# Two blocks' shared down projection as seven-product pairs, and first-block weight mixes moved to a later place

## What is computed

```python
xn = _layernorm(x)
# part 1: of each token's 2752 gate values the half that is smallest in size is set to zero
s = silu(einsum('bsh,ih->bsi', xn, w_gate))           # I = 2752
_, idx = top_k(-abs(s), int(0.5 * I))
s = s with those positions set to 0, times einsum('bsh,ih->bsi', xn, w_up)
part1 = einsum('bsi,hi->bsh', s, w_down)              # 1024 wide
# part 2
h = relu(einsum('bsh,hi->bsi', xn, up_w)) ** 2        # hidden, 2048 wide
shared_out = einsum('bsi,ih->bsh', h, down_w)         # the shared down projection
latent = einsum('bsh,hl->bsl', xn, fc1_w)             # 512 wide
routed_out = einsum('bsl,lh->bsh', einsum('bsl,lm->bsm', latent, expert_w) * sum_of_top2, fc2_w)
part2 = layernorm(shared_out + routed_out) * gamma + beta
return x + part1 + part2
```

## Time and profile before

| | us |
|---|---|
| median of 3 runs (lowest, highest) | 2308.17 (2308.01, 2308.75) |
| the profiled execution | 2309.1 |
| its span in the profile | 2307.3 |

### The profile page before, as it was taken

One profiled execution on the slowest core, in us unless ns is written; L12 is line 12 of the kernel. 1 busy time (PEld: TensorE's weight loads), 2 busy tenths in 40 slices (PEclk: granted clock), 3 DMA queues, 4 the chain that ended last, 5 costly groups with the idle time before them and its releaser, 6 DMA issues.

```text
span 2307.3 us, 27055 instructions
## 1 busy us (share of the span) xinstructions
PE 2286.7 (99%) x10360; PEld 1902.2 (82%) x10360; DVE 1155.0 (50%) x1496; ACT 698.2 (30%) x1093; POOL 890.7 (39%) x662
## 2 busy tenths in 40 slices
PE   8989999999999999999999999999999999999999
PEld 6878888888888888888888888888888888888887
DVE  4432667757334457607434544932823544690560
ACT  3233554223333326201114323510212432531110
POOL 5445656677445533133015452223203445204300
PEclk9999999999999999999999999999999999999999
DMA  7999999868888876557668887557667888755755
GB/s 267 338 396 395 347 364 334 301 212 298 295 288 282 272 282 234 194 192 273 213 232 295 270 291 278 195 195 259 223 222 252 270 281 292 246 193 195 272 191 179
DMA packets 213411, 611.88 MB, mean 265 GB/s; under 512 B 22304, under 2 KB 31520, under 8 KB 210208
## 3 DMA queue, kind: packets, MB, share of 16 engines
q1 hardware_dynamic: 213280, 610.13, 76.1%
HBM read 466.32 MB, written 143.72 MB: 264 GB/s over the span
## 4 chain that ended last, share of the span: by engine, by line
PE 93%; DMA 3%; DVE 2%; SPq 1%; ACT 1%; issue 0%; POOL 0%; DVEq 0%; ACTq 0%
PE bank L1107 30%; PE bank L1109 30%; PE bank L1108 30%; PE bank L1127 2%; DMA mixed_w<-mixes 2%; DMA raw<-w_gate_dram 1%; PE bank L1118 1%; DMA w<-mixed_w 0%; DMA split_w<-w 0%; SPq L667 0%; DVE positive L1368 0%; SPq L663 0%; PE bank L1201 0%; PE bank L1200 0%; DVE mixes L1317 0%
## 5 line engine op out<-in xcount | busy, mean ns | idle before, releaser
L886 POOL TENSOR_TENSOR w<-raw,w 128x512 fp32r<-128x512 f32 (+1 forms) x196 | 281.8, 1446 | 203.6 <-ACT w L930 203.2
L1107 PE MATMUL bank<-w,prod_t 128*128 128x512 f32 x672 | 269.4, 401 | 0.0
L1109 PE MATMUL bank<-w,prod_t 128*128 128x512 f32 x672 | 262.9, 391 | 0.0
L1108 PE MATMUL bank<-w,prod_t 128*128 128x512 f32 x672 | 262.0, 390 | 0.0
L1107 PE MATMUL bank<-w,tok 128*128 128x512 f32 (+1 forms) x664 | 254.1, 383 | 6.9 <-POOL w L886 6.0
L1109 PE MATMUL bank<-w,tok 128*128 128x512 f32 (+1 forms) x664 | 253.2, 381 | 0.0
L1108 PE MATMUL bank<-w,tok 128*128 128x512 f32 (+1 forms) x664 | 253.2, 381 | 0.0
L1108 PE MATMUL bank<-tok,w 128*128 128x512 f32 x640 | 249.0, 389 | 0.0
L1109 PE MATMUL bank<-tok,w 128*128 128x512 f32 x640 | 249.0, 389 | 0.0
L1107 PE MATMUL bank<-tok,w 128*128 128x512 f32 x640 | 249.0, 389 | 0.0
L891 POOL TENSOR_TENSOR w<-w 128x512 fp32r<-128x512 f32 x114 | 167.5, 1492 | 183.0 <-ACT w L1069 182.8
(11 more groups left out here) (175 smaller groups left out, 4334.0 us busy)
## 6 DMA issues: line engine op xcount, KB each, us to landing
w<-split_w SPq DMA_DIRECT2D x480, 512.0 KB, 4.2
split_w<-w SPq DMA_DIRECT2D x184, 512.0 KB, 5.9
w<-mixed_w SPq DMA_DIRECT2D x144, 256.0 KB, 3.3
w_more<-split_w SPq DMA_DIRECT2D x72, 512.0 KB, 5.1
w_more<-mixed_w SPq DMA_DIRECT2D x96, 256.0 KB, 3.7
rows<-x_dram SPq DMA_DIRECT2D x32, 512.0 KB, 5.2
mixed_w<-own SPq DMA_DIRECT2D x12, 1024.0 KB, 6.5
spilled_u<-prod SPq DMA_DIRECT2D x12, 1024.0 KB, 8.0
```

Source lines behind the costliest of these rows:

```text
L886: pool.tensor_tensor(lo, words, hi, ALU.subtract).then_inc(lo_ready, 1)
L1107: pe.matmul(out, left[0], right[0], start=first, stop=False)
L1108: pe.matmul(out, left[0], right[1], start=False, stop=False)
L1109: return pe.matmul(out, left[1], right[0], start=False, stop=last)
```

## The change

1. In blocks 2 and 3 (`WIDE`) the shared down projection becomes two pairs, 5 and 6, by seven products in an order of their own (`SHARED_PRODUCTS`). Latent and routed come before them. The granules of such a block after the fifth pair: latent 148, hidden 0 at 156, routed 164 and 168, hidden 1 at 172, pair 5 at 180 to 207, hidden 2 and 3 at 208 and 216, pair 6 at 224 to 251, out 252 to 295. A pair's left operands are the hidden values of two groups: the even one gives A11 (and, with its other half, S1), the odd one A12 and A22. ACT cuts them out of PSUM (`cut_units`), DVE multiplies by the relu (`make_units`) and forms S1 to S4, ACT makes high halves (`upper_units`, `upper_early_sum`, `upper_late_sums`), POOL the low halves (`lower_units`), and DVE adds the seven products into `acc` (`read_shared`, 28 adds of 512 columns a pair). T4's low half is made on DVE. A product with 48 fewer matmuls a block results: 336 instead of 384. The search steps, the pick, the masks, the gated products, the turns of the last chunks, and the loads of spilled up values are placed anew.
2. Eight new mixed sets for these pairs are made in block 1, at granules 158 + 7 i: loads, `mix_shared` on DVE at + 5, store at + 6.
3. In block 0 the twelve own sets move from granules 4 + 11 i to 44 + 9 i; mix at + 5 and store at + 6 instead of + 6 and + 7. gamma and beta are loaded at granule 158 instead of 142.

The core of the diff:

```diff
 PAIRS = [(("gate", 0), ("gate", 1)), (("gate", 2), ("gate", 3)), (("gate", GC - 2), ("up", GC - 2)),
-         (("up", 0), ("up", 1)), (("up", 2), ("up", 3))]
+         (("up", 0), ("up", 1)), (("up", 2), ("up", 3)),
+         (("shared", 0), ("shared", 1)), (("shared", 2), ("shared", 3))]
 
 FAST = [0, 5, 5, 5]
+WIDE = [False, False, True, True]
+SHARED_PAIRS = [5, 6]
 FIRST_PAIRS = 2
 UP_PAIR, SPILLED = 2, (3, 4)
 PRODUCTS = ["A11 B11", "S2 T2", "A12 B21", "S1 T1", "S4 B22", "S3 T3", "A22 T4"]
+SHARED_PRODUCTS = ["A11 B11", "S3 T3", "A12 B21", "A22 T4", "S1 T1", "S2 T2", "S4 B22"]
+SHARED_TARGETS = {"A11 B11": (11, 12, 21, 22), "S3 T3": (21, 22), "A12 B21": (11,), "A22 T4": (21,),
+                  "S1 T1": (12, 22), "S2 T2": (12, 21, 22), "S4 B22": (12,)}
...
+_WIDE_STEPS = [*_middle[:2], *_middle[3:5], _middle[2], SHARED_PAIRS[0], *_middle[7:9], SHARED_PAIRS[1], *_last[-2:]]
...
+                for n, p in enumerate(SHARED_PAIRS):
+                    even, odd = (end[("hidden", 2 * n + i)] for i in range(2))
+                    begun = self.start[("hidden", 2 * n + 1)]
+                    self.units_cut_at.update({even + 2: (n, 0), odd + 8: (n, 1)})
+                    self.units_at.update({even + 2: (n, 0), odd + 1: (n, 1)})
+                    self.early_sum_at[begun + 2] = n
+                    self.units_hi_at.update({begun + 3: (n, 0), odd + 8: (n, 1)})
+                    self.early_hi_at[begun + 4] = n
+                    self.late_hi_at[odd + 9] = n
+                    self.units_lo_at.update({begun + 5: (n, "early"), odd + 8: (n, "A12"), odd + 10: (n, "A22"),
+                                             odd + 12: (n, "S1"), odd + 15: (n, "S2"), odd + 19: (n, "S4")})
...
-        self.search_end = steps_at[COUNTS + 1] + 3 * TILES + 1
-        self.pick_at = {steps_at[COUNTS + 1] + 3 * t: t for t in range(TILES)}
-        self.pick_from = steps_at[COUNTS + 1]
+        self.pick_from = self.start[("hidden", 2)] + 1 if wide else steps_at[COUNTS + 1]
+        self.search_end = self.pick_from + (2 if wide else 3) * TILES + 1
+        self.pick_at = {self.pick_from + (2 if wide else 3) * t: t for t in range(TILES)}
...
-OWN_FROM = {n: 4 + 11 * i for i, n in enumerate(OWN_SETS)}
+OWN_FROM = {n: 44 + 9 * i for i, n in enumerate(OWN_SETS)}
 OWN_LOADS = {at + i: (n, i) for n, at in OWN_FROM.items() for i in range(4)}
-OWN_AT = {at + 6: n for n, at in OWN_FROM.items()}
-OWN_STORES = {at + 7: n for n, at in OWN_FROM.items()}
-FIRST_NORM_LOAD = 142
+OWN_AT = {at + 5: n for n, at in OWN_FROM.items()}
+OWN_STORES = {at + 6: n for n, at in OWN_FROM.items()}
+FIRST_NORM_LOAD = 158
...
+SHARED_FROM = {n: 158 + 7 * i for i, n in enumerate(SHARED_SETS)}
+SHARED_LOADS = {at + i: (n, i) for n, at in SHARED_FROM.items() for i in range(4)}
+SHARED_AT = {at + 5: n for n, at in SHARED_FROM.items()}
+SHARED_STORES = {at + 6: n for n, at in SHARED_FROM.items()}
...
 def vector_makes(granule):
 
-    return PRODUCTS[granule.key[2]] == VECTOR_LO and granule.key[1] < SPILLED[0]
+    _, p, q = granule.key
+    return products(p)[q] == VECTOR_LO and (p < SPILLED[0] or p in SHARED_PAIRS)
...
+            def load_shared_mix(n, i):
+
+                p, k = n // HALF, n % HALF
+                if n > SHARED_SETS[0]:
+                    sp.wait_ge(shared_stored, 16 * (n - SHARED_SETS[0]))
+                else:
+                    sp.wait_ge(bank_filled, filled(1, ("fast", FAST[1] - 1, len(PRODUCTS) - 1, 1)))
+                src, width = words_of((PAIRS[p][i // 2], k + i % 2 * HALF))
+                sp.dma_start(shared_own[:, i, :], src).then_inc(shared_loaded, 16)
+
+            def store_shared_mix(n):
+                sp.wait_ge(shared_mixes, 4 * (n - SHARED_SETS[0]) + 4)
+                sp.dma_start(mixed_w[n].rearrange("i p n -> p i n"), shared_own[:, :, :]).then_inc(shared_stored, 16)
...
+                    elif n in SHARED_SETS:
+                        sp.wait_ge(shared_stored, 16 * (n - SHARED_SETS[0] + 1))
...
+            def lower_units(b, n, what):
+
+                at = shared_round(b, n)
+                if what == "early":
+                    hi, lo = UNIT_SLOT["A11"]
+                    pool.wait_ge(unit_summed, at * UNIT_SUMS + 1)
+                    pool.wait_ge(operand_hi, highs(b, "hidden", (2 * n + 1) * TILES))
+                    pool.tensor_tensor(unit_r[:, lo, :, :], unit_raw[:, lo, :, :], unit_r[:, hi, :, :],
+                                       ALU.subtract).then_inc(units_lo, 1)
+                    hi, lo = SUM_SLOT["S3"]
+                    pool.wait_ge(unit_sum_hi, at * UNIT_HIS + 1)
+                    pool.tensor_tensor(unit_sums_r[:, lo, :, :], unit_sums[:, EARLY_RAW, :, :], unit_sums_r[:, hi, :, :],
+                                       ALU.subtract).then_inc(units_lo, 1)
+                elif what == "A12":
+                    hi, lo = UNIT_SLOT[what]
+                    for k in range(HALF):
+                        pool.wait_ge(unit_summed, at * UNIT_SUMS + 1 + 2 * k + 2)
+                        pool.wait_ge(operand_hi, highs(b, "hidden", (2 * n + 1) * TILES + k + 1))
+                        pool.tensor_tensor(unit_r[:, lo, k, :], unit_raw[:, lo, k, :], unit_r[:, hi, k, :],
+                                           ALU.subtract).then_inc(units_lo, 1)
...
+            def cut_units(b, n, odd):
+
+                if n == 0 and not odd:
+                    for c in range(4):
+                        act.wait_ge(spilled[c], 16 * b)
+                for k in range(HALF):
+                    words = banks[bank_of(b, ("hidden", 2 * n + odd, k))][:, :].rearrange("p (h n) -> p h n", h=2)
+                    act.wait_ge(bank_filled, filled(b, ("hidden", 2 * n + odd, k)))
+                    act.activation(unit_raw[:, 3:6:2, k, :] if odd else unit_raw[:, 1:8:6, k, :], words,
+                                   ACT.Relu).then_inc(units_cut, 1)
+
+            def upper_units(b, n, odd):
+
+                for k in range(HALF):
+                    act.wait_ge(units_made, shared_round(b, n) * 2 * HALF + odd * HALF + k + 1)
+                    hi, words = ((unit_r[:, 2:5:2, k, :], unit_raw[:, 3:6:2, k, :]) if odd else
+                                 (unit_r[:, 0, k, :], unit_raw[:, 1, k, :]))
+                    act.activation(hi, words, ACT.Copy).then_inc(operand_hi, 1)
...
+                if p in SHARED_PAIRS:
+                    n = SHARED_PAIRS.index(p)
+                    if granule.opens or left == "A12":
+                        pe.wait_ge(units_lo, unit_lo(b, n, (left, k) if left == "A12" else left))
...
+            def make_units(b, n, odd):
+
+                at = shared_round(b, n)
+                for k in range(HALF):
+                    bank = bank_of(b, ("hidden", 2 * n + odd, k))
+                    words = banks[bank][:, :].rearrange("p (h n) -> p h n", h=2)
+                    out = unit_raw[:, 3:6:2, k, :] if odd else unit_raw[:, 1:8:6, k, :]
+                    dve.wait_ge(units_cut, at * 2 * HALF + odd * HALF + k + 1)
+                    dve.scalar_tensor_tensor(out=out, in0=words, scalar=0.0, in1=out, op0=ALU.max,
+                                             op1=ALU.mult).then_inc(bank_emptied[bank], 1)
+                    value = emptied(b, ("hidden", 2 * n + odd, k))[1]
+                    dve.wait_ge(bank_emptied[bank], value)
+                    dve.sem_inc(units_made, 1)
+                if not odd:
+                    return
+                a12, a22, s3 = unit_raw[:, 3, :, :], unit_raw[:, 5, :, :], unit_sums[:, EARLY_RAW, :, :]
+                s4 = unit_sums[:, SUM_SLOT["S4"][1], :, :]
+                dve.wait_ge(units_lo, unit_lo(b, n, "S3"))
+                for k in range(HALF):
+                    dve.tensor_tensor(s3[:, k, :], a22[:, k, :], s3[:, k, :], ALU.subtract).then_inc(unit_summed, 1)
+                    dve.wait_ge(unit_summed, at * UNIT_SUMS + 1 + 2 * k + 1)
+                    dve.tensor_tensor(s4[:, k, :], a12[:, k, :], s3[:, k, :], ALU.subtract).then_inc(unit_summed, 1)
+                dve.tensor_tensor(unit_raw[:, 7, :, :], unit_raw[:, 7, :, :], a22, ALU.add).then_inc(unit_summed, 1)
...
+            def read_shared(b, p, q):
+
+                for j in range(2):
+                    bank, value = emptied(b, ("fast", p, q, j))
+                    dve.wait_ge(bank_filled, filled(b, ("fast", p, q, j)))
+                    if q or p > SHARED_PAIRS[0]:
+                        added = ("fast", p, q - 1, j) if q else ("fast", p - 1, 6, j)
+                        added_bank, added_value = emptied(b, added)
+                        dve.wait_ge(bank_emptied[added_bank], added_value)
+                    targets = SHARED_TARGETS[SHARED_PRODUCTS[q]]
+                    for target in targets:
+                        t, i = j + 2 * (target // 20), target % 10 - 1
+                        if p == SHARED_PAIRS[0] and q == 0:
+                            other, other_value = emptied(b, ("routed", i, t))
```

(4 more changed lines are left out.)

203 lines of the change are left out of this document (174 added, 29 removed).

## The result

The changed kernel takes 2346.10 us (median of 4 runs, 2344.37 to 2348.38) against 2308.09 of the kernel before (4 runs): a ratio of 1.0164, 95% interval 1.0151 to 1.0177. The forecast was 2308.9, with 2291 to 2325 as its range.

What follows compares the result with a forecast made beforehand. PE, busy 99%, was taken to bound the kernel: 2309.1 - 21.8 (matmuls) + 28 (four pairs) - 6.5 (block 0) + 1 (block 1) = 2309.8, less 0.9 to the median, 2308.9 us; range 2291 to 2325.

Steps and rivals of the forecast that it cites:

- Matmuls, -21.8: Shared down projection of the two wide blocks: 96 fewer matmuls at 0.2267 us each, -21.8 us, all on PE's path.
- T4's wait, 5.1 at first: Near granule 12 of each pair: PE waits for T4's low half, 3.7 to 6.5 us, taken as 5.1.
- E+22.8: Latest T4 time in a pair, counted from PE ending hidden 1 or 3; a wait of 6.5 us.
- My step that ACT's queue sets T4's time: Pair start: ACT's odd cut stands behind four mixed splits, free at about E+6.2, starting the chain to T4 at E+20.0.
- The second gap, 1.9: Between the second and third T4 low half DVE reads four banks: 1.1 to 2 us more, 1.9 taken per pair.
- the two don't add: In a pair, the second gap and half clock overlap, because a slow PE also needs T4's third low half later.
- 1.3 inside the same wait: Pair 6: six gated products on POOL, about 8.3 us, delay A12's low halves some 1.3 us, inside T4's wait.
- The out stage at nothing: Rest of the wide block, outside the pairs, costed at nothing; no term for the out stage.
- Block 0, -6.5: Moved own sets: -8.7 us of early waits and half clock, +1.2 near granule 154, +1 for stores; range -10.5 to 0.
- Block 1, +1: Eight shared sets through DVE and SP at granules 158 to 213 cost +1 us, range 0 to 5.
- B: Slower rival: POOL and DVE collide at every pair, half clock after each wait; 9.5 a pair, 38; 2318.9 us; chance 0.24.
- E's block 0: Slower rival through SP: stores hold SP, block 0 gives back nothing, block 1 loses 5; 2319.4 us; chance 0.05.

Runs made afterwards that it cites:

- no_gated: Changed kernel, with the six gated products on POOL ahead of pair 6 cut to one column of each unit group: 2340.37 us.
- out_late: Changed kernel, with loads of spilled up values 1 to 3 issued earlier and the out stage's normalisation of part 2 two granules later: 2337.25 us.

## Why the prediction was wrong

The time came out 37 us above the forecast. By place, against the sum: the out stage 17.6 more, the four pairs 11.4 more, block 0 7.5 more, block 1 1.6 less. Three steps failed: the out stage costed at nothing, the gated products counted inside T4's wait, and block 0's gain taken as net.

- **Matmuls, -21.8: right.** 96 fewer, and the count of matmuls in the trace shows it.
- **T4's wait, 5.1 at first: too large.** 3.5 wherever nothing hid it, under the 3.7 that I had as the least. The cuts came 1.7 us earlier than I worked out from the first phase's loads, and the sums took 1.3 more than their free price. My upper end was also added up wrongly: E+22.8 leaves out the 0.8 by which I let T4's own low half grow, so it should have been E+23.6 and a wait of 7.3. My step that ACT's queue sets T4's time was wrong in weight: taking it away gave 7.3 us where 18 to 25 were expected, because sums and T4 low halves then stood longer beside POOL's operations (8.4 and 5.36 us).
- **The second gap, 1.9: one wait missed.** The third T4 low half cost PE 1.3 us, as forecast (1.1 to 2). The second, for which the sum had nothing, cost 1.1 in three of the four pairs: it took 2.88 us beside the whole of S2's low half, where I had up to 1.5. Pair 5 lost 7.5 and 8.8 instead of 7.0; "the two don't add" held, as half clock followed in block 3 and not in block 2.
- **The gated products ahead of pair 6, "1.3 inside the same wait": failed.** They are a wait of their own at granule 228, 6.9 and 7.1 us with half clock. I took them as starting at their due granule 221; they started 8 us later, behind masks that stand behind the pick, and the pick's buffer lies over extra slots that pair 5 uses. The queue ahead of POOL was read, the chain ahead of that queue was not. That they make this wait is shown (no_gated); that a start on time would have avoided it is read from the trace and was not run.
- **The out stage at nothing: failed, the largest item (17.6).** I named the cover for the search and the reads, but costed the spread loads of spilled values and the masks behind them at zero without following the masks to the variance, the square root and ACT's copies. With the loads earlier and the normalisation later, 11.2 of the 17.6 went (out_late).
- **Block 0, -6.5: failed, +1.0.** The early waits went in full (9.7). Against it, the late set held SP until 454.4 (455 forecast) and the weights were ready at 463.2 (463.3 forecast), so that chain was right; but I took PE's arrival, 462.07, from the trace before, though the sum itself brings PE there 8.7 us sooner. PE came at 460.1, and with 1.6 of half clock the place lost 4.7 instead of 1.2. Two mixes in places where DVE feeds PE or ACT were not looked for (4.1 and 1.9).
- **Block 1, +1: small, as said.** 0.6 less was lost than before, outside the range of 0 to 5 but within what its small waits differ by from run to run.
- **Rivals.** B's size for the pairs was met (38 forecast, 7.5 + 8.8 + 11.5 + 11.6 = 39.4 measured), but that is luck in part: 14 of it is the place at granule 228 and not the collision with half clock that B is about. E's block 0 that gives back nothing came true, though SP accounts for 4.7 of the 10.7 us there. The range was missed by what no rival had: 17.6 us in the out stage and 8.5 more than forecast in block 0's later waits.

By the Trainium skill (page "SBUF — State Buffer", section "Who interferes with whom") a DVE operation with two SBUF inputs and a GpSimd operation that reads SBUF exclude each other, and the later one waits for the whole of the other. The runs agree: two T4 low halves took 5.36 us beside whole operations and 1.83 beside pieces.

## What to carry to other kernels

When work is moved onto engines that had room on average, add up each engine's work in the stretch itself and follow every queue one step further back: who starts the first instruction in it, and when. A wait taken away where several engines are full only shows the next one, so count lost time by place, not single waits. An edit that "costs nothing" needs its chain written down as much as one that costs.
